# Filler transposes in TensorE's first gaps, and the first convolution ahead of the statistics of unit 4 on VectorE

## What is computed

```python
# block 1, xn = layernorm(x)
K   = C_vec * sigmoid(A_param)**t * B_vec              # one decaying filter per channel
out = causal_conv(xn, K) + D_vec * xn                  # along the 256 tokens of a sequence
out = gelu(out) @ W_proj.T + b_proj
x   = x + layernorm(layernorm(xn + out) * gamma + beta)
# block 2, t = layernorm(x), t_prev = t shifted by one token
r   = sigmoid((mu_r*t + (1-mu_r)*t_prev) @ W_r.T)
k   = relu((mu_k*t + (1-mu_k)*t_prev) @ W_k.T)**2
x   = x + layernorm(r * (k @ W_v.T))
```

## Time and profile before

| | |
|---|---|
| median of 3 runs | 155.37 us (154.94 to 155.74) |
| the profiled execution's own time | 156.3 us |
| its span, first to last instruction | 153.7 us |
| mean granted clock of TensorE | 0.976 |
| busy: PE, DVE, ACT, POOL | 139.1, 131.8, 130.1, 131.2 us |

### The profile page before, as it was taken

The page is one execution under the profiler, slowest core; times in us unless marked ns, Lnnn a source line. Parts: engine busy times, 40 slices in busy tenths (PEclk is TensorE's granted clock), DMA queues, the critical chain, the costliest instruction groups (busy, mean ns, idle before and its releaser), DMA issues.

```text
span 153.7 us, 3286 instructions
## 1 busy us (share of the span) xinstructions
PE 139.1 (91%) x957; PEld 119.2 (78%) x957; DVE 131.8 (86%) x373; ACT 130.1 (85%) x387; POOL 131.2 (85%) x194
## 2 busy tenths in 40 slices
PE   3879998999999999999999999999999999999600
PEld 3769897989697888879977899789797788777500
DVE  1979999999999999999999699997999996333773
ACT  5749789899969899979899999779989988999800
POOL 4598959999989899999899979978889989999880
PEclk9978999999999999999999999999999999999995
DMA  3889900000000002000200002200200000422743
GB/s 91 209 227 313 339 22 2 0 0 6 0 0 0 0 4 73 0 0 0 71 1 0 0 4 70 69 4 4 68 0 0 0 0 4 139 68 68 236 134 108
DMA packets 18704, 8.98 MB, mean 58 GB/s; under 512 B 1536, under 2 KB 18688, under 8 KB 18688
## 3 DMA queue, kind: packets, MB, share of 16 engines
q1 hardware_dynamic: 18400, 8.79, 19.6%
q10 hardware_dynamic: 288, 0.00, 0.1%
HBM read 4.59 MB, written 4.19 MB: 57 GB/s over the span
## 4 chain that ended last, share of the span: by engine, by line
PE 69%; POOL 9%; ACT 6%; DVE 4%; DMA 3%; SPq 3%; issue 3%; DVEq 0%; POOLq 0%; ACTq 0%
PE ps_r L734 9%; PE ps_r L733 9%; PE ps_k L722 8%; PE ps_k L723 8%; PE ps_tv L742 8%; PE ps_z L700 7%; PE ps_prefix L683 6%; PE ps_tv L713 5%; PE ps_z L701 3%; DMA x_all<-in_x 3%; ACT xn L323 3%; PE ps_prefix L685 3%; PE ps_xT L676 3%; POOL x_r L201 2%; POOL xn_pow L214 2%
## 5 line engine op out<-in xcount | busy, mean ns | idle before, releaser
L323 ACT ACTIVATE xn<-x_all,x_bias,x_r 128x128 f32<-128x128 f32 x64 | 26.3, 489 | 2.4 <-POOL x_bias L203 2.4
L734 PE MATMUL ps_r<-mixed_T,tsT 128*128 128x128 f32 x128 | 24.7, 275 | 0.0
L733 PE MATMUL ps_r<-mixed_T,tsT 128*128 128x128 f32 x128 | 24.7, 275 | 0.0
L380 ACT ACTIVATE f_normal<-f,out_bias,yf_r 128x128 f32<-128x128 f32 x56 | 22.9, 492 | 0.5 <-POOL out_bias L256 0.5
L214 POOL TENSOR_TENSOR xn_pow<-xn,pow_token 128x512 f32<-128x512 f32 x16 | 20.4, 1278 | 3.1 <-ACT xn L323 2.1
L700 PE MATMUL ps_z<-pv_T,gelu 128*128 128x128 f32 x128 | 22.3, 276 | 0.3 <-DVE pv_T L566 0.2
L733 PEld LDWEIGHTS ps_r<-mixed_T,tsT 128*128 128x128 f32 x128 | 19.6, 192 | 1.4 <-issue 1.4
L683 PE MATMUL ps_prefix<-prefix_ones,xn_pow 128*128 128x256 f32 x64 | 19.7, 391 | 0.8 <-POOL xn_pow L214 0.8
L343 ACT ACTIVATE junk<-ps_z 128x128 f32<-128x128 f32 x64 | 16.7, 276 | 3.9 <-PE ps_z L701 3.8
L700 PEld LDWEIGHTS ps_z<-pv_T,gelu 128*128 128x128 f32 x128 | 19.3, 191 | 0.7 <-DVE pv_T L566 0.4
L495 DVE SCALAR_TENSOR_TENSOR x_all<-ps_z,yf_r,x_all 128x128 f32<-128x128 f32 x64 | 17.6, 341 | 2.6 <-POOL yf_r L235 2.5
(11 more groups left out here) (92 smaller groups left out, 367.1 us busy)
## 6 DMA issues: line engine op xcount, KB each, us to landing
out_x<-x_all SPq DMA_DIRECT2D x15, 256.0 KB, 2.3
x_all<-in_x SPq DMA_DIRECT2D x7, 512.0 KB, 6.0
x_all<-in_x SPq DMA_DIRECT2D x2, 128.0 KB, 3.0
x_all<-in_x SPq DMA_DIRECT2D x1, 256.0 KB, 3.5
out_x<-x_all SPq DMA_DIRECT2D x2, 128.0 KB, 1.8
w_pv<-in_W_proj SPq DMA_DIRECT2D x1, 64.0 KB, 2.7
w_pv<-in_W_v SPq DMA_DIRECT2D x1, 64.0 KB, 4.0
w_rk<-in_W_r SPq DMA_DIRECT2D x1, 64.0 KB, 3.6
```

Of the source, the lines that this page charges most:

```text
L323: last = a_.activation(tile(xn[u % D], j), xa(u, j), ACT.Identity, bias=col(x_bias, u, j), scale=col(x_r, u, j))
L380: last = a_.activation(tile(f_normal[u % D], j), tile(f[u % D], j), ACT.Identity, bias=out_bias[:, u, j:j + 1], scale=yf_r[:, u, 1, j:j + 1])
L733: t_.matmul(tile(ps_r, j), tsT[u % D][:, q, l + 1:l + 1 + P], mixed_T[:, 0, :], start=True, stop=False)
L734: last = t_.matmul(tile(ps_r, j), tsT[u % D][:, q, l:l + P], mixed_T[:, 1, :], start=False, stop=True)
```

## The change

The order of calls changes on two engines, and nothing else. On VectorE `convolve(0)` comes before `x_stats(4)` and no longer behind it. On TensorE two calls of fillers are added, `keep_busy(6)` before the transposes of unit 0 and `keep_busy(8)` between them and the first prefix sum.

```diff
-            x_stats(2); x_pooled(2, 2); make_mixers(); x_stats(4); convolve(0); x_pooled(4, 2); keep_pv()
+            x_stats(2); x_pooled(2, 2); make_mixers(); convolve(0); x_stats(4); x_pooled(4, 2); keep_pv()
...
             centre_bias()
-            transpose_xn(0); prefix_sum(0); keep_busy(8); transpose_rk(); transpose_pv(); transpose_xn(1)
+            keep_busy(6); transpose_xn(0); keep_busy(8); prefix_sum(0); keep_busy(8); transpose_rk(); transpose_pv(); transpose_xn(1)
```

## The result

The changed kernel took 154.86 us (median of 20 runs, 154.59 to 155.48), the kernel before, run beside it, 155.33 us (20 runs, 154.83 to 156.07). The ratio is 0.9973, with a 95% interval of 0.9960 to 0.9986. So the change makes the kernel 0.14 to 0.4% faster. That is a real gain and a small one, inside the 0.5% that I had called the limit of a measurement; the forecast was 154.9 us, with a change of less than 0.5% as the likeliest verdict.

The account below looks back on a forecast made before the run. TensorE was taken to bound the kernel from some 34 us, so only an earlier start counts: 0.48 us at t_scaled(0), taken from the median 155.37, gives 154.9 us; range 154.1 to 155.8.

Parts of the forecast that it names:

- The first prefix sum at full clock: TensorE's first prefix sum, with fillers holding the clock, ends at 10.58 instead of 11.39, 0.81 us earlier.
- So they cost nothing: Fourteen added fillers on TensorE fit its gaps at full clock: six in 0.66 of 0.67 us, eight in 0.88.
- The 1.6 us: At low clock the fourteen fillers take 3.1 us in TensorE gaps of 1.5, so up to 1.6 us late; none charged.
- The first stall: VectorE's x_neg of unit 4, held by GpSimd's xn_pow, comes before it; project(0) starts at 15.00 instead of 15.88.
- No part does this alone: With only the fillers or only the new order, x_neg of unit 4 still asks at 14.26 or 14.27.
- The second stall: VectorE's x_neg of units 6 and 7 asks 0.16 us after xn_pow(3) begins and is held to 18.32, about 1 us.
- This stall is moved and not removed: The stall of about 1 us comes again at VectorE's later x_neg; gamma_z(0) starts near 18.49 instead of 18.76.
- The sum: t_scaled(0), ACT's scaling of unit 0, goes from 32.99 to 32.51, 0.48 us, giving 154.9 us; chance 0.50.
- (A): Rival: x_neg of unit 6 is served before xn_pow(3) or held shorter; 0.98 us kept, 154.4 us; chance 0.24.
- (B): Rival: fillers don't hold the clock; first prefix sum ends at 11.39 again, x_neg stalls; 155.4 us; chance 0.13.
- (C): Rival: the low clock comes one stretch later, in TensorE's gaps near 11.4 or 13.1; 156.2 us; chance 0.08.
- The rule weighed in the prediction: Transposes don't count as TensorE being busy, so fillers wouldn't hold the clock; by it the sum is nothing.

Follow-up runs that it names:

- experiment 8: The changed kernel itself, unaltered, timed again on another chip: 154.71 us, ratio 0.9942 to the kernel before.
- Experiment 6: The changed kernel plus two more statistics of unit 4 into an unread scratch tile before x_neg: 155.30 us, ratio 0.9981 to the kernel before.
- experiment 1: The kernel before plus the two calls of fillers, VectorE's order left as before: 155.27 us, ratio 0.9984.
- experiment 2: The kernel before with convolve(0) ahead of the statistics of unit 4, no fillers added: 154.96 us, ratio 0.9985.
- experiment 5: The kernel before with the load of units 4 and 5 issued ahead of W_proj and W_v, no fillers, old order: 155.02 us, ratio 0.9958.
- experiment 3: The changed kernel with the statistics of unit 8 drawn ahead of x_v and x_neg of units 6 and 7: 154.97 us, ratio 0.9986 to the kernel before.
- experiment 4: Experiment 3's kernel with the load of units 6 and 7 issued ahead of gamma and beta: 154.74 us, ratio 0.9970 to the kernel before.
- experiment 7: Experiment 3's kernel with two one-column memsets more near the start of VectorE's program: 154.47 us, ratio 0.9913 to the kernel before.
- experiment 10: Experiment 7's kernel, all fillers kept, with the load of units 6 and 7 ahead of gamma and beta: 154.44 us, ratio 0.9942 to the kernel before.
- experiment 9: Experiment 7's kernel without the fourteen added fillers: 155.17 us, ratio 0.9967 to the kernel before.
- the last version: Experiment 10's kernel with three and four added fillers instead of six and eight: 154.53 us, ratio 0.9943 to the kernel before.

## Why the prediction was right, and where it was not

**The first prefix sum at full clock: right, 0.20 us late.** The forecast was an end at 10.58, measured was 10.78. The term that was mis-sized is "So they cost nothing". I took the six fillers to begin at 6.86 and to run at full clock, as the trace of before had the bias product over by then. In the changed kernel's trace they began at 7.17 and took 0.99 us, 0.83 from their start to that of the next instruction where I had 0.66: the transposes of unit 0 were 0.47 us late and the prefix sum 0.29. In experiment 8 it was 0.8. The 1.6 us that I gave as the price without cover was the right thing to weigh, and I should have charged a part of it.

**The first stall gone: right, and for the reason given.** x_neg of unit 4 asked at 13.65 (forecast 13.46), before the xn_pow at 13.96 (14.07), and project(0) started at 14.89 (15.00) with no wait. Experiment 6 shows that this is the gain in span: put x_neg back behind the xn_pow with the order and the fillers kept, and every execution is long. The margin was 0.31 us where I had 0.61, small enough for slow fillers to undo it (experiment 8).

**"No part does this alone": wrong as a general statement.** It is right for the execution that I had read. But units 4 and 5 landed at 11.41 there and at 10.84 in experiment 1, and the clock fell in that execution and not in nine of the 12 of experiment 2. Of 90 executions of the kernel before, 29 had a mean clock of 0.976 or less, and 26 of these had a long span; of the other 61, 42 had. So what the change does is to move odds: long spans in 68 of 90 before, in 6 of 30 with the change (4 of 20 and 2 of 10). The fillers' share in this is that none of 108 executions with them had a clock of 0.976 or less (the lowest was 0.977), against 8 of 36 without them where the kernel was otherwise edited, all 8 in experiments 2 and 5. I set that bound after I had seen the runs. The order's share is that VectorE's statistics no longer stand ahead of the convolution.

**The second stall: right in place and mechanism, its size off.** I had x_neg of unit 6 asking at 17.35, held to 18.32. It asked at 17.88, 0.80 us after the xn_pow and not 0.16, and was held to 18.20, 0.32 us. The missed term is the transfer of units 6 and 7: I took its 4.8 us to land as fixed, so 13.76 and no wait, and it took 6.1 us, to 15.04. The wait of 0.75 us came out of time that the stall would have taken anyway, so that the end hardly moved: gamma_z(0) started at 18.36 (forecast 18.49). "This stall is moved and not removed" held.

**The sum: right, in part by luck.** 0.48 us was forecast, 0.47 measured between the medians, 0.4 to 0.5 between the median spans of the changed kernel (153.1) and those of before on the other chips (153.5 or 153.6). But 0.48 was worked out for one execution with the stall, and the pair of profiled executions shows 0.67; about 0.1 of it is that GpSimd's own chain ran 0.11 earlier in the second (13.96 against 14.07). A median over both heaps is another quantity, and that it came out the same isn't something that the prediction argued. It also carried the profiled execution's 156.3 - 153.7 = 2.6 us outside the span over to the changed kernel (155.8 round 153.2), that is, it put this term at no change. Measured was 154.86 - 153.0 = 1.86 there and never more with all fourteen fillers. In the mean the kernel before had 155.54 us in its 90 executions and the changed one 154.91 in its 30: 0.30 of the difference is span and 0.33 lies outside it.

**The rivals.** (A), no second stall, didn't happen by itself. Experiments 3 and 4 used its time though x_neg was still held 0.23 and 0.24 us, and in experiment 7 it was free. That was worth 0.27 us at L713 (33.38), 0.50 with the transfer, where I had given it 0.5 for 154.4 us; 154.47 and 154.44 us were measured for experiments 7 and 10. (B), a late first prefix sum and the stall back, came by another road than its own in the one long execution of the changed kernel that has a trace, experiment 8: the granted clock didn't fall, the fillers themselves were late. Five more of the 30 were long, without a trace. (C), a fall that comes later, was seen in no trace. The rule weighed in the prediction, that transposes don't count as TensorE being busy (the Trainium skill, "TensorE: Matmul & The Clock Gate", "Part 4: PE-mode transpose"), isn't borne out here: with transposes in the gaps the window of 9.7 to 13.1 had a granted clock of 1.00, against 0.51 before, and none of the 108 executions with fillers had a low mean clock. The counts carry this and not the one window, which read 1.00 in the trace of experiment 9 too, without new fillers.

**What stays open.** What the engines do outside the span, and why all fourteen fillers, and not half of them, keep that time short; what lets the clock fall in some executions without the fillers and not in others (in none of the 12 of experiment 9); why the gate at 104.8 is late in experiments 3 and 4; that five executions of experiment 3 had spans of 153.4 to 154.1 us, of which no trace was taken; and what part of the last version's gain is the memsets and what the rest, since they weren't tried by themselves on the changed kernel.

## What to carry to other kernels

Where a short VectorE instruction now and then takes about a microsecond, set its start against the GpSimd instruction that began last: here asking 0.01 us after it began cost 1.1 us and asking 0.31 before it nothing, so move it by some tenths, with work or a transfer, and leave margin, since transfers and the first matmuls vary by more. Judge such a change by many executions and not by one pair of traces, and by two numbers for each: the span, which a timeline can explain, and the own time less the span, which here moved by up to 1.2 us and hid in the medians. Weigh fillers by their time at half speed as well, at which a part of them ran here: all fourteen could make the first prefix sum 0.8 us late, and yet half of them, which kept all 12 spans short, left 3 of 12 executions with the longer time outside the span.

## What the runs showed of the hardware that I had not expected

- How early TensorE runs at full speed differs between executions. The bias product behind the first eighteen fillers took 0.28 us in the trace of before and 0.43 in that of the changed kernel; the six fillers took 0.99 and 1.51 us in two traces of the changed kernel. The granted clock doesn't show it: from 6.3 to 9.7 it read 1.00 in both of these, and from 2.5 to 6.3, where a filler takes 0.22 us, it read 1.00 as well. Only the durations do.
- The transfer of units 6 and 7, 512 KB at the same place of the program, landed at 13.76 in the trace of before (issue and 4.8 us), while the statistics that wait for it could start only at 15.04, 14.75 and 14.39 in those of the change and of experiments 1 and 3.
- The hold of VectorE by GpSimd ended 1.12 to 1.15 us after the start of the 1.27 us instruction in ten traces.
- An execution's time outside its span was 1.69 to 1.86 us in all 96 executions with fourteen more fillers, and up to 2.9 us without them, at no difference in the mean granted clock.
- An instruction of VectorE started 0.36 us after its releaser in two kernels and at once in the others, and it was gone in the four traces with two memsets more at the start of VectorE's program.
